# Values products of query tiles 5 and 6, and of 7 and 8, issued as one run each

## The reference

```
q_latent, kv_latent = x @ wq_down, x @ wkv_down           # ranks 192 and 64
q = [q_latent @ wq_nope, rope(q_latent @ wq_rope)]         # 16 heads, 128 + 64
k = [kv_latent @ wk_nope, rope(kv_latent @ wk_rope)]
probs = softmax(mask(q k^T / sqrt(192)))                   # causal, 1024 x 1024
out = (probs @ (kv_latent @ wv_up)) @ wo
```

## Time and profile before

| what | value |
|---|---|
| median of 3 runs (1143.56 to 1144.35) | 1143.94 us |
| the profiled execution's own time | 1144.08 us |
| its span, first to last instruction | 1142.3 us |
| TensorE matmul busy (PE) | 1106.8 us, 97% |
| weight loads (PEld), VectorE, ScalarE, GpSimd busy | 80%, 65%, 56%, 43% |
| mean granted TensorE clock | 0.994 of full speed |

### The profile page before, as it was taken

The page is one execution under the profiler, slowest core; times in us unless marked ns, Lnnn a source line. Parts: engine busy times, 40 slices in busy tenths (PEclk is TensorE's granted clock), DMA queues, the critical chain, the costliest instruction groups (busy, mean ns, idle before and its releaser), DMA issues. The chain is left out here.

```text
span 1142.3 us, 22436 instructions
## 1 busy us (share of the span) xinstructions
PE 1106.8 (97%) x7360; PEld 911.9 (80%) x7360; DVE 739.5 (65%) x1556; ACT 635.2 (56%) x1285; POOL 490.8 (43%) x384
## 2 busy tenths in 40 slices
PE   6989999999999999999999999899999999999997
PEld 3668888888888888888888887688888878888885
DVE  6878778678688687687787765454444445444444
ACT  3575766766766767667766676443434333343332
POOL 1265456466466456446546552033333332333332
PEclk9999999999999999999999999899999999999999
DMA  6100000000000000010000021273333334433332
GB/s 221 56 19 19 3 18 20 1 18 18 0 17 19 0 18 18 0 36 0 0 18 0 1 66 30 84 222 110 115 110 115 110 107 131 118 117 110 115 105 92
DMA packets 26309, 67.85 MB, mean 59 GB/s; under 512 B 3028, under 2 KB 9428, under 8 KB 26264
## 3 DMA queue, kind: packets, MB, share of 16 engines
q1 hardware_dynamic: 26120, 67.24, 19.5%
q10 hardware_dynamic: 144, 0.07, 0.0%
HBM read 62.82 MB, written 4.47 MB: 59 GB/s over the span
## 5 line engine op out<-in xcount | busy, mean ns | idle before, releaser
L838 ACT ACTIVATE prob<-ps_s,nm 128x128 f32<-128x128 f32 (+7 forms) x256 | 189.5, 740 | 164.8 <-DVE nm L998 162.9
L1436 POOL TENSOR_TENSOR hl<-hf,hh 128x512 fp32r<-128x512 f32 x96 | 123.4, 1286 | 295.4 <-ACT hh L1373 295.4
L998 DVE CUSTOM_DVE_ANT_0 ps_s<-ps_s,causal 128x128 f32<-128x128 f32 (+7 forms) x256 | 195.5, 764 | 55.0 <-PE ps_s L653 47.5
L664 PE MATMUL ps_t<-ident,prob 128*128 128x128 f32 x1152 | 177.5, 275 | 4.3 <-ACT pt L848 3.0
L664 PEld LDWEIGHTS ps_t<-ident,prob 128*128 128x128 f32 x1152 | 136.5, 140 | 30.4 <-issue 11.4
L679 PE MATMUL ps_o<-pt,kvn 128*64 128x128 f32 x2304 | 154.0, 278 | 0.5 <-DVE pt L1007 0.4
L679 PEld LDWEIGHTS ps_o<-pt,kvn 128*64 128x64 f32 x2304 | 123.2, 136 | 33.3 <-issue 21.3
L1405 DVE TENSOR_TENSOR gs<-gs,routing 128x512 f32<-128x512 f32 x64 | 44.3, 692 | 137.8 <-ACT gs L1369 137.8
L1007 DVE COPY pt<-ps_t 128x128 f32<-128x128 f32 (+2 forms) x192 | 102.0, 531 | 48.3 <-PE ps_t L664 46.4
L1373 ACT ACTIVATE hh<-hf 128x512 fp32r<-128x512 f32 x96 | 60.7, 633 | 121.6 <-DVE hf L1410 121.6
L1369 ACT ACTIVATE gs<-ps_g 128x512 f32<-128x512 f32 x96 | 57.4, 598 | 121.4 <-PE ps_g L1328 121.4
(11 more groups left out here) (291 smaller groups left out, 2560.2 us busy)
## 6 DMA issues: line engine op xcount, KB each, us to landing
routing<-wT_scratch SPq DMA_DIRECT2D x34, 256.0 KB, 3.7
raw_a<-in_e SPq DMA_DIRECT2D x17, 384.0 KB, 3.1
cosv<-in_e SPq DMA_DIRECT2D x17, 384.0 KB, 3.0
sinv<-wT_scratch SPq DMA_DIRECT2D x17, 384.0 KB, 3.6
raw<-in_e SPq DMA_DIRECT2D x17, 384.0 KB, 3.0
routing<-wT_scratch SPq DMA_DIRECT2D x16, 384.0 KB, 3.3
raw_a<-in_a SPq DMA_DIRECT2D x8, 512.0 KB, 3.3
raw_b<-in_b SPq DMA_DIRECT2D x8, 480.0 KB, 3.8
```

Source lines behind the costliest of these rows:

```text
L664: mm = nc.tensor.transpose(ps_t[x][:, at * P:(at + 1) * P], prob[t % 2][e][:, j * P:(j + 1) * P], ident[:, :])
L838: nc.scalar.activation(prob[t % 2][e][:, 0:len(halves) * width].rearrange("p (h k) -> p h k", k=width), ps_s[e][:, 0:len(halves), 0:width] ...
L998: nc.vector.tensor_tensor_reduce(out=s_ps, in0=s_ps, in1=bias, scale=-1.0, scalar=-MASKED, op0=ALU.add, op1=ALU.min, accum_out=nm[:, e:e + ...
L1436: nc.gpsimd.tensor_tensor(hl[:, c, :], hf[:, c, :], hh[:, c, :].bitcast(F32), ALU.subtract).then_inc(h_lo, 1)
```

## The change

Probabilities no longer go to two buffers by parity but to one area with a place for every tile (`places`, in blocks of 128), and the copies wait by a table (`area_free`) for the tiles that shared their place. TensorE no longer multiplies tile 4 in step 6, but ahead of tile 5 in step 7; and no longer tile 6 in step 0, but ahead of tile 7 in step 1. Around this, `WA` moves from the end of step 6 to behind the values of step 7, `Y0` to behind the turns of (6,e1), `QR0` ahead of the second score of step 0. On VectorE `split_a` moves behind the copy of (6,e0) and the addition of Y0 behind the copy of (6,e1). The end of the stage gets the order of step 0 and 1. To make room, the routing's scratch `rest` shares the tensor `w2`, and the causal mask is kept with 640 columns in place of 1024, read with an overlapping pattern for tiles in two halves.

```
--- before.py
+++ after.py
@@ -480,9 +480,10 @@
         qhi, qlo = ([keep[f"q{w}0"], [ctx.enter_context(nc.sbuf_tensor(f"q{w}1{e}", [P, T], F32R)) for e in range(2)]] for w in ("hi", "lo"))
         cosv, sinv, ident, raw_a, raw_b = (keep[n] for n in ("cosv", "sinv", "ident", "raw_a", "raw_b"))
         causal, rhi, rlo, lhi, llo = (keep[n] for n in ("causal", "rhi", "rlo", "lhi", "llo"))
-        rest, shifted, top, total = tensors(nc, ctx, [
-            ("rest", [P, NT, E], F32), ("shifted", [P, NT, E], F32), ("top", [P, NT, 8], F32), ("total", [P, NT], F32)])
+        shifted, top, total = tensors(nc, ctx, [
+            ("shifted", [P, NT, E], F32), ("top", [P, NT, 8], F32), ("total", [P, NT], F32)])
         logits, w2 = keep["logits"], keep["w2"]
+        rest = w2
         bhi, blo = tensors(nc, ctx, [("bhi", [P, 256], F32R), ("blo", [P, 256], F32R)])
 
         sh = keep["xtf"][:, :, :].rearrange("p k (g c) -> p (k g) c", c=CH)
@@ -492,7 +493,9 @@
         wst = t1[0:E, :, :].rearrange("p g c -> p (g c)")
 
         prob = [[ctx.enter_context(nc.sbuf_tensor(f"prob{par}{e}", [P, (TILES - 1 + par) * P], F32)) for e in range(2)] for par in range(2)]
-        pt = [ctx.enter_context(nc.sbuf_tensor(f"pt{par}", [P, 2, TILES - 1 + par, P], F32)) for par in range(2)]
+        area = ctx.enter_context(nc.sbuf_tensor("pt", [P, sum(2 * (t + 1) for t in (4, 5, 6)) * P], F32))
+        places = [16, 18, 22, 28, 0, 10, 22, 0]
+        pt = [area[:, places[t] * P:(places[t] + 2 * (t + 1)) * P].rearrange("p (e j q) -> p e j q", e=2, q=P) for t in range(TILES)]
         nm, lsum, linv = tensors(nc, ctx, [("nm", [P, 2], F32), ("lsum", [P, 2, TPC, 2], F32), ("linv", [P, 2, TPC, 2], F32)])
         yacc = keep["yacc"]
         bank = lambda name: ctx.enter_context(nc.psum_tensor(name, [P, CH], F32))
@@ -551,6 +554,10 @@
                 return w_rows, int(name[1]) + 1
             return y_added, (s * 4 + int(name[1]) + 1 if name[1] != "p" else (s - 1) * 4 + 2 + int(name[2]) + 1)
 
+        def area_free(s, t):
+
+            return 2 * (s * TILES + (-2, -2, 0, 0, 0, 2, 4, 6)[t])
+
         @block.sync
         def _(sp):
             with sp.Fori(0, PAIRS - 1) as i:
@@ -676,7 +683,7 @@
                 at = slice(t % TPC * P, (t % TPC + 1) * P)
                 for j in range(t + 1):
                     for e in range(2):
-                        mm = nc.tensor.matmul(ps_o[64 * e:64 * e + 64, at], kvn[:, b * 8 + j, :], pt[t % 2][:, e, j, :], start=j == 0, stop=j == t)
+                        mm = nc.tensor.matmul(ps_o[64 * e:64 * e + 64, at], kvn[:, b * 8 + j, :], pt[t][:, e, j, :], start=j == 0, stop=j == t)
                         if j == t:
                             mm.then_inc(pv_done, 1)
 
@@ -752,15 +759,16 @@
 
                         def products():
                             if earlier or t > 1:
+                                if t in (1, TILES - 1):
+                                    values(*before_tile(i, b, t, 3))
                                 values(*before_tile(i, b, t, 2))
 
                         if t == 0:
                             scores(i, b, t, 0, 0)
                             turns(0)
-                            products()
+                            also("QR0")
                             scores(i, b, t, 1, 0)
                             turns(1)
-                            also("QR0")
                         elif t == 1:
                             scores(i, b, t, 0, 0)
                             products()
@@ -795,27 +803,30 @@
                             turn(sp, tp, 0, 1)
                             if t < TILES - 1:
                                 also(("L0", "QL1")[t - TPC - 1])
-                            products()
+                            if t != TPC + 2:
+                                products()
+                            if t == TILES - 1:
+                                also("WA")
+                            scores(i, b, t, 1, 0)
+                            turns(1)
                             if t == TILES - 1:
                                 also("Y0")
-                            scores(i, b, t, 1, 0)
-                            turns(1)
                             scores(i, b, t, 1, 1)
-                            also(("B", "WA", "Y1")[t - TPC - 1])
+                            if t != TPC + 2:
+                                also("B" if t == TPC + 1 else "Y1")
 
             for name in PROLOGUE[3:]:
                 project(0, None, name, 0, 0)
             pairs_loop(pe, body)
 
             s, t = 2 * PAIRS - 1, TILES - 1
-            for g in range(2):
-                turn(s, t, 0, g)
-            values(s, 1, t - 1)
-            for g in range(2):
-                turn(s, t, 1, g)
+            for e in range(2):
+                for g in range(2):
+                    turn(s, t, e, g)
             pe.wait_ge(widened, s * 2 + 2)
             pe.wait_ge(y_added, s * 4 + 2)
             spread(ps_x).then_inc(misc_ready, 1)
+            values(s, 1, t - 1)
             values(s, 1, t)
             pe.wait_ge(olo_done, 2 * s + 2)
             for m, out in enumerate((ps_x, ps_t[0])):
@@ -844,8 +855,8 @@
                 before = s * TURNS_PER_S + turns_before(t) + (e if t >= TPC else 0)
                 blocks = groups_of(t)[g]
                 act.wait_ge(turned[0], before + 1)
-                ge(act, pv_done, 2 * (s * TILES + t - 1))
-                nc.scalar.activation(pt[t % 2][:, e, blocks[0]:blocks[-1] + 1, :].rearrange("p j q -> p (j q)"),
+                ge(act, pv_done, area_free(s, t))
+                nc.scalar.activation(pt[t][:, e, blocks[0]:blocks[-1] + 1, :].rearrange("p j q -> p (j q)"),
                                      ps_t[0][:, 0:len(blocks) * P], ACT.Copy).then_inc(copied[0], 1)
 
             def widen(s, c):
@@ -994,7 +1005,12 @@
                 halves = halves_of(t)
                 dve.wait_ge(scores_ready, s * U + 2 * t + e + 1)
                 s_ps = ps_s[e][:, 0:len(halves), 0:halves[0][1]]
-                bias = causal[:, T - (t + 1) * P:T].rearrange("p (h k) -> p h k", k=halves[0][1])
+                width = halves[0][1]
+                bias = causal[:, CH + P - width:CH + P].rearrange("p (h k) -> p h k", h=1)
+                if len(halves) == 2:
+
+                    bias = causal[:, CH - width:CH]
+                    bias = bass.AP(bias.tensor, bias.offset, [bias.ap[0], (P, 2), (1, width)])
                 nc.vector.tensor_tensor_reduce(out=s_ps, in0=s_ps, in1=bias, scale=-1.0, scalar=-MASKED, op0=ALU.add, op1=ALU.min,
                                                accum_out=nm[:, e:e + 1]).then_inc(max_done, 1)
 
@@ -1003,8 +1019,8 @@
                 before = s * TURNS_PER_S + turns_before(t) + (e if t >= TPC else 0)
                 blocks = groups_of(t)[g]
                 dve.wait_ge(turned[1], before + 1)
-                ge(dve, pv_done, 2 * (s * TILES + t - 1))
-                nc.vector.tensor_copy(pt[t % 2][:, e, blocks[0]:blocks[-1] + 1, :].rearrange("p j q -> p (j q)"),
+                ge(dve, pv_done, area_free(s, t))
+                nc.vector.tensor_copy(pt[t][:, e, blocks[0]:blocks[-1] + 1, :].rearrange("p j q -> p (j q)"),
                                       ps_t[1][:, 0:len(blocks) * P]).then_inc(copied[1], 1)
 
             def invert(s, c):
@@ -1048,8 +1064,6 @@
                             add_out(misc(i, b, "Yp1"), ps_x, s - 1, 1 - b, 1, 1)
                         if t == TPC + 2 and b == 0:
                             split_b(i, b)
-                        if t == TPC + 3 and b == 0 and not is_last(i):
-                            split_a(i, b, i + 1)
                         maximum(s, t, 0)
                         if has and (t == 0 or t > TPC):
                             take_turned(sp, tp, 0, 1)
@@ -1068,8 +1082,8 @@
                             normalise(s, 0)
                         if more and t == TPC + 2:
                             latent_low(i, b, 1, s + 1, 1 - b)
-                        if t == TPC + 3:
-                            add_out(misc(i, b, "Y0"), ps_x, s, b, 0, 0)
+                        if t == TPC + 3 and b == 0 and not is_last(i):
+                            split_a(i, b, i + 1)
                         if t == 0:
                             maximum(s, t, 1)
                             if has:
@@ -1077,7 +1091,9 @@
                         else:
                             if t > TPC:
                                 take_turned(sp, tp, 1, 1)
-                            else:
+                            if t == TPC + 3:
+                                add_out(misc(i, b, "Y0"), ps_x, s, b, 0, 0)
+                            if t <= TPC:
                                 take_turned(sp, tp, 1, 0)
                             maximum(s, t, 1)
                         if t == 1 and earlier:
@@ -1459,7 +1475,7 @@
         keep["w_loaded"] = [ctx.enter_context(nc.semaphore(f"w_loaded{q}")) for q in range(SLOTS)]
```

(6 more changed lines are left out.)

30 lines of the change are left out of this document (20 added, 10 removed).

## The result

The changed kernel takes 1158.45 us (median of 4 runs, 1156.15 to 1160.93), the kernel before 1143.75 us beside it (4 runs): ratio 1.0135, 95% interval 1.0116 to 1.0155. It is 14.7 us slower; the forecast was 15.6 us slower.

What follows compares the result with a forecast made beforehand. TensorE was taken to bound the kernel. Costs of 12.2 + 2.8 + 12.2 + 2.0 = 29.2 us less 13.6 gained made +15.6 us, 1159.5 us; range 1145 to 1165.

Steps and rivals of the forecast that it cites:

- What bounds the kernel: Attention rounds: TensorE, busy 595.46 of 600 us from 100 to 700 us, so any new wait on it is paid in full.
- The join costs nothing: Where two values runs meet on TensorE: taken as 0, bounded by a whole boundary of 0.34 us, 31 times.
- Rival 4: Joined values runs pay a boundary again: 31 x 0.34 = 10.5 us more, 1170 us; chance 0.07.
- The gain: TensorE's rounds: spared values runs 5.1 and 4.4 us, Y0 0.7, turn of (7,e0) 3.4; 13.6 us saved.
- The score of (7,e0): Step 7: waits 0.71 us for ScalarE's exponential of (6,e0) behind QL1; with slower first matmul 12.2 us over 15 rounds.
- Rival 3: Faster: the step 7 score of (7,e0) does not wait; with no collision either, 1136 us; chance 0.10.
- split_a ahead of the addition: VectorE, seven b=0 rounds: split_a delays Y0's addition, so Y1 waits 1.65 us, 1.75 with refill; 12.2 us.
- the collision: b=0 rounds: VectorE's rhi and rlo crawl beside GpSimd's qlo pair, rlo ending 0.41 us after it; missing it saves 9.8 us.
- Rival 1: rhi and rlo miss GpSimd's operations, or the pair comes earlier: 1149.7 us; chance 0.20.
- Y0, then Y1: Same bank: Y1 waits 0.25 us for VectorE's addition of Y0, 0.35 with refill, in eight rounds; 2.8 us.
- QR0 ... at most 0.1 us x 8, taken as 0: Step 0: QR0, ahead of the second score, needs Y1's addition, expected within 0.1 us of its turn; no cost charged.
- The end: Last round and stage end: tile 4 costs 0.85 us in step 7, tile 6 ahead of tile 7 1.1; together 2.0 us.

Runs made afterwards that it cites:

- e9: e8 with Y0 and its addition back directly behind the values in rounds without WA (b=1 and the last b=0 round): 1133.42 us, ratio 0.9902 to the kernel before.
- e4: Changed kernel with only tile 6 joined to tile 7; tile 4, WA, Y0, split_a and Y0's addition as in the kernel before: 1142.76 us, ratio 0.9999.
- e6: Changed kernel with the edits of e1 and e2 together: 1139.01 us, ratio 0.9966 to the kernel before.
- e2: Changed kernel with rhi and rlo, the raw_a half of split_a, done by VectorE in step 5 of b=0 rounds: 1151.07 us, ratio 1.0067.
- e3: Changed kernel with GpSimd's qlo pair of the b=0 rounds waiting until VectorE has written rlo: 1150.56 us, ratio 1.0066.
- e1: Changed kernel with step 6 reordered: ScalarE's exponential of (6,e0) ahead of QL1's halves, VectorE's maximum of (6,e1) ahead of QL1's low part: 1154.90 us, ratio 1.0104.
- e8: e6 without the joins at the edges: tile 4 in step 6 in the second and last round, tile 6 between the end's turns: 1134.31 us, ratio 0.9905.
- e5: The order of e7 with the edits of e1 and e2, without the joins at the edges: 1165.71 us, ratio 1.0180 to the kernel before.
- e7: Changed kernel with both joins, but WA, Y0, split_a and Y0's addition where the kernel before has them: 1152.72 us, ratio 1.0073.

## Why the prediction was right, point by point

- **What bounds the kernel.** TensorE, and a new wait on it is paid in full: it idles 13.0 us more from 100 to 700 us, and the first to eighth B are 14.2 us further apart.
- **The join costs nothing.** 44 issues in 2.56 us and 60 in 3.43 (361.64 to 365.07) are 44 and 60 times 0.055 plus one end of 0.14, to 0.01 us. Rival 4 is out.
- **The gain.** The forecast's terms make 1.84 us a pair (two runs of 0.34, two of 0.29, 0.1 at Y0, 0.49 at the turn; seven times 0.11 at Y0 is 0.8 and not the 0.7 of the sum, which changes nothing). In e9 a pair is 1.35 us shorter than before, with 0.28 (QR0) and 0.35 (Y1, b=0) of waits still in it: 1.98. That agrees with what was read from the rows, though e9 has other moves in it too; of a single run saved only the late one was measured by itself (0.33 in e4's b=0 round).
- **The score of (7,e0).** Forecast 0.71 us of wait and 0.10 on the first matmul; measured, the score was due at 303.85 (303.65, its predecessor's last product, and 0.20) and came at 304.56, 0.71, and its first product took 0.34 in place of 0.23. It came in 14 of the 15 rounds with QL1; in the second round the turn ahead of it waits 2.15 us and leaves nothing to wait for (below). That it is a term by itself is shown by e6 against e2: 12.1 us, forecast 12.2. Rival 3 is out.
- **split_a ahead of the addition.** The chain came as worked out: from the score's start T, rhi at T + 6.9 (forecast 6.7), the qlo pair T + 6.0 to 8.6 (6.1 to 8.7), rlo's end T + 9.05 (9.1), Y1 T + 10.17 (10.35). The wait is 1.39 us and not 1.65: the copy and the addition ran 0.1 us shorter than summed, and TensorE was ready 0.1 us later. One reading was off without harm: rhi takes 0.63 us in the median and not the 1.34 of the earlier trace rows, since here it meets the pair's first operation near its end; rlo is held to the pair's end either way. By e2 and e3 the collision is worth 7.4 and 7.9 us. Rival 1 is out. The Trainium skill, "SBUF — State Buffer", Who interferes with whom, lets whichever engine issues first hold the port for a whole instruction. The rows agree as to who waits: GpSimd's two operations began at 352.72 and 354.07, ahead of rhi (353.58) and of rlo (354.24), and it was VectorE that took longer; in e1's first pair rlo began first (91.52, the pair at 91.86) and kept its 0.56 us, and GpSimd's pair took 2.74 us in place of 2.64.
- **Y0, then Y1: a term wrongly set apart.** The wait is there as forecast (0.25 us, 0.10 behind it), but e9 took it away in the b=1 rounds and won 0.10 us. "QR0 ... at most 0.1 us x 8, taken as 0" is the step that failed: QR0 needs Y1's addition, and it came free only because Y1 had already waited. The 2.8 us are the price of either.
- **The end**: +3.7 us from the eighth B to the experts. The forecast has 2.5 for this stretch: 2.0 for the end, and 0.5 for the last round with b=0, which has no WA (0.81 + 0.35 - 0.34 - 0.29). The rest is clock, which the forecast left out. The last turn waits 1.95 us, and behind it the clock is at its lower level (0.56 granted from 739.10 to 742.50):

```profile
739.08 1.56 PE L671 MATMUL ps_t<-ident,prob 128*128 128x128 f32 x8 [1.95 <-ACT pt L859]
```

  From there to the last output products (747.89) TensorE takes 8.81 us, and 7.19 in e6 at full clock: 1.6 us. The other way, the kernel before has such a stretch at the start of the experts (0.51 granted from 730.0 to 736.8 us), and after it is not there: 0.5 us ahead of the experts (730.02 to 732.59, against 748.69 to 750.74) and the 1.25 in them.
- **Not in the forecast: the first pair.** It lost 5.2 us where the later ones lost 1.5. Y1 waited there, and a turn of the second round too (131.96, 2.15 us, against 0.71 at that place before): VectorE has the routing's weights to do, which tile 4's values had covered (in e8, with tile 4 back in step 6, the wait is 0.71 again). TensorE's two longest waits of that pair, with what comes behind the first:

```profile
96.98 0.47 PE L713 MATMUL ps_x<-ohi,bhi 128*128 128x512 f32 x1 [2.02 <-DVE yacc L1042]
...
98.25 1.93 PE L671 MATMUL ps_t<-ident,prob 128*128 128x128 f32 x8
...
131.96 0.87 PE L671 MATMUL ps_t<-ident,prob 128*128 128x128 f32 x3 [2.15 <-DVE pt L1023]
```

  Behind both the clock was at its lower level (0.57 and 0.51 in the stretches of the first fence). That alone cost 1.4 us behind the first (3.45 us from 98.25 in place of 2.05) and 1.5 behind the second (4.77 us to the next values run, 3.23 in e6).

So the steady pairs lost less than forecast, 1.50 against 1.87 us each, mostly the shorter wait of Y1; the first pair and the end lost more. The total is nearer than its parts deserve: these errors have opposite signs. Of the profiled execution's 16.9 us the lower clock made 4.5 (1.4, 1.5 and 1.6), and 1.8 went the other way; without either it would be about 14.2 us, an estimate from these rows, against the 15.6 forecast. The mechanisms, though, are those named, and with both waits removed and the edges left as they were the joins give 10 us.

## What to carry to other kernels

When work moves out from between two steps, ask of each step behind it what that work had covered: here tile 4's values covered the exponential behind QL1, QL1's bank for WA, and the routing's work on VectorE, and each showed as a wait once the values had gone. Two waits close together are not priced one by one, since the second can take what the first gives back (e1 alone 3.5 us, beside e2 12.1). And VectorE's operations on SBUF alone are to be placed by what GpSimd does at that time, not by their place in the list only: beside GpSimd's pair rhi and rlo were 1.25 us longer.

## What was not expected of the hardware

A wait on TensorE can cost more than itself. Behind idle times of 1.82 us (e1, steady rounds), 1.95, 2.02 and 2.15 (changed kernel) and 2.51 (e5) its rows run at half pace for some 3.4 us, 1.4 to 1.6 us lost each time: the eight turns and QR0 take 3.45 us from 98.25 and 3.66 in e1, against 2.05 at full clock. Behind the 1.23 us of the steady rounds of the changed kernel it stays at full clock. It does not always fall. Behind the 1.83 us of e1 it fell in five rounds of six (not at 181.08); behind the turn's 2.15 us in three of the six kernels that have this wait (the changed kernel, e2 and e7; not e1, e3 and e6, where the three turns take 0.52 us in place of 0.87); behind the 2.5 us of e5 in six rounds of seven (not at 440.39). So the length of the wait alone does not decide it, and what else does was not tried.
